# Product-key experts mixed by halves of the tokens, with the up products of the first half among the mixing of the second

## What is computed

```python
def _L0_ffn_ref(x, w_q, keys, expert_down, expert_up, norm_w):
    H, DK, K = (8, 128, 8); NKEYS = 64; NEXP = NKEYS * NKEYS
    xn = _rmsnorm(x, norm_w)
    q = (xn @ w_q.T).reshape(b, t, H, 2, DK)
    sim1 = jnp.einsum('bthd,hkd->bthk', q[..., 0, :], keys[:, :, 0, :])
    sim2 = jnp.einsum('bthd,hkd->bthk', q[..., 1, :], keys[:, :, 1, :])
    s1, i1 = jax.lax.top_k(sim1, K)
    s2, i2 = jax.lax.top_k(sim2, K)
    all_idx = (i1[..., :, None] * NKEYS + i2[..., None, :]).reshape(b, t, H, K * K)
    all_sc = (s1[..., :, None] + s2[..., None, :]).reshape(b, t, H, K * K)
    fs, pk = jax.lax.top_k(all_sc, K)
    fi = jnp.take_along_axis(all_idx, pk, axis=-1)
    wd, wu = expert_down[fi], expert_up[fi]
    hidden = jax.nn.gelu(jnp.einsum('btd,bthkd->bthk', xn, wd), approximate=False)
    hidden = hidden * jax.nn.relu(fs)
    return jnp.einsum('bthk,bthkd->btd', hidden, wu)
```

## Time and profile before

| | us |
|---|---|
| median of 3 runs | 486.81 (485.98 to 500.19) |
| the profiled execution, its own time | 488.01 |
| its span in the trace | 486.2 |
| PE busy | 453.0 (93%) |
| DVE busy | 285.0 (59%) |
| ACT busy | 180.9 (37%) |
| mean granted clock of PE | 0.965 of 2.4 GHz |

### The profile page before, as it was taken

How to read it: one execution, slowest core, us unless ns; L and a number is a source line. 1 busy time by engine, 2 the same in 40 slices (tenths; PEclk the granted TensorE clock), 3 DMA queues, 4 the chain that set the end, 5 groups by cost and what they waited for, 6 DMA issues and landing times.

```text
span 486.2 us, 8648 instructions
## 1 busy us (share of the span) xinstructions
PE 453.0 (93%) x3217; PEld 320.0 (66%) x3217; DVE 285.0 (59%) x967; ACT 180.9 (37%) x444; POOL 6.4 (1%) x9
## 2 busy tenths in 40 slices
PE   4999999999999899978899899899899999979997
PEld 3645555455455588856758788788646778767774
DVE  7266676676667654787689889500336554435243
ACT  2446665755665602777223220000024333223110
POOL 4000000000000000000000000000000000000000
PEclk9999999999999999999999995689899999988999
DMA  8400001000004906100089278000291000000000
GB/s 296 141 2 2 0 1 45 1 0 0 0 0 160 359 6 266 82 1 1 2 263 329 74 239 195 0 0 1 51 379 54 0 1 1 0 1 1 0 1 22
DMA packets 21694, 36.20 MB, mean 74 GB/s; under 512 B 1696, under 2 KB 18209, under 8 KB 21025
## 3 DMA queue, kind: packets, MB, share of 16 engines
q1 hardware_dynamic: 21664, 35.82, 22.9%
HBM read 35.55 MB, written 0.26 MB: 74 GB/s over the span
## 4 chain that ended last, share of the span: by engine, by line
issue 44%; PE 37%; DVE 15%; ACT 2%; POOL 1%; DVEq 0%; DMA 0%; POOLq 0%
PE bank L824 6%; PE bank L985 6%; PE bank L890 4%; PE bank L865 3%; PE bank L870 2%; PE bank L999 2%; PE bank L814 1%; DVE region_a L1538 1%; PE bank L879 1%; DVE region_a L1596 1%; PE bank L793 1%; PE bank L1003 1%; DVE region_a L1535 1%; DVE region_g L1604 1%; PE bank L382 1%
## 5 line engine op out<-in xcount | busy, mean ns | idle before, releaser
L1062 ACT ACTIVATE region_g<-bank,nm_new 128x512 f32<-128x512 f32 x64 | 43.4, 683 | 40.8 <-DVE nm_new L1326 40.0
L1321 DVE CUSTOM_DVE_ANT_0 bank<-bank,bias_h 128x512 f32<-128x512 f32 x64 | 43.0, 713 | 7.5 <-issue 7.5
L526 PEld LDWEIGHTS bank<-ident,region_g 128*128 128x128 f32 x264 | 28.2, 140 | 24.8 <-issue 12.1
L526 PE MATMUL bank<-ident,region_g 128*128 128x128 f32 x264 | 36.2, 280 | 0.8 <-ACT region_d L1043 0.8
L543 PE MATMUL bank<-region_d,region_a 128*64 128x256 f32 x288 | 35.0, 385 | 0.0
L566 PE MATMUL bank<-region_a,qT 64*128 64x512 f32 x128 | 34.7, 618 | 0.0
L324 ACT ACTIVATE root<-var 128x2 f32<-128x2 f32 x6 | 1.2, 203 | 84.0 <-DVE var L334 84.0
L824 PE MATMUL bank<-region_u,region_g 128*128 128x256 f32 x128 | 30.4, 403 | 1.5 <-issue 1.5
L1043 ACT COPY region_d<-bank 128x512 f32<-128x512 f32 x50 | 27.6, 587 | 11.0 <-PE bank L526 11.0
L824 PEld LDWEIGHTS bank<-region_u,region_g 128*128 128x128 f32 x128 | 26.0, 204 | 5.6 <-issue 1.6
L814 PE MATMUL bank<-region_a 64*128 64x32 bf16 x768 | 27.2, 249 | 2.2 <-DVE region_a L1596 2.2
(11 more groups left out here) (317 smaller groups left out, 807.4 us busy)
## 6 DMA issues: line engine op xcount, KB each, us to landing
region_d<-in_downT SPq DMA_DIRECT2D x2, 2048.0 KB, 10.2
region_u<-in_up SPq DMA_DIRECT2D x2, 2048.0 KB, 12.3
region_a<-in_ctx SPq DMA_DIRECT2D x1, 3072.0 KB, 16.1
region_d<-in_w_q SPq DMA_DIRECT2D x1, 2048.0 KB, 12.2
region_d<-in_ctxT SPq DMA_DIRECT2D x1, 2048.0 KB, 9.9
region_d<-in_ctxT SPq DMA_DIRECT2D x2, 1024.0 KB, 16.0
region_u<-in_wg SPq DMA_DIRECT2D x1, 1728.0 KB, 8.2
region_u<-in_wu SPq DMA_DIRECT2D x1, 1728.0 KB, 13.2
```

Source lines behind the costliest of these rows:

```text
L526: mm = nc.tensor.transpose(bank[4 + e][:, k * P:(k + 1) * P], prob[:, u % 2, e, k * P:(k + 1) * P], ident[:, :])
L1062: nc.scalar.activation(prob[:, u % 2, e, :], bank[2 * s + e][:, :], ACT.Exp, scale=-1.0, bias=nm_new[:, p, t, e:e + 1], accum_out=l_blk[:, ...
L1321: ins = nc.vector.tensor_tensor_reduce(bank[2 * s + e][:, :], bank[2 * s + e][:, :], bias_h[:, t, :], -1.0, 3e38, ALU.add, ALU.min, accum_ ...
```

## The change

A pass now makes the weights of 32 tokens of one tile: the upper 64 rows of the array take 16 tokens of that tile's first 64, the lower rows the 16 that lie 64 later. So passes 1 to 4 finish token tile 0 and passes 5 to 8 tile 1. For this `chosen` holds each token's 64 entries twice, the turning takes six transposes into two banks, and `chosenT` is copied by two instructions on 64 partitions each.

On PE passes 1 to 4 stay in a loop. Then PE waits until tile 0 is weighed, and passes 5 to 8 are written out with seven up products of tile 0 in each (`BESIDE = 7`): two after every 24 mixing matmuls, one after the last 24. Four up products of tile 0 and the 32 of tile 1 follow; before those of tile 1 PE waits for the last weighing.

On DVE the three multiplications by score pieces become one instruction on 1536 elements, the two of `weigh` one on 1024; the eight passes are written out, and the one-hots of pass 2 come ahead of the wait for the GELU.

```diff
+HALF = P // GS // 2
+BESIDE = 7
...
-        chosen = part(region_a, 3584, 3 * P).rearrange("p (s n) -> p s n", s=3)
+        chosen = part(region_a, 3584, 6 * P).rearrange("p (s t c n) -> p s t c n", s=3, t=TT, c=2)
...
                     for k in range(3):
-                        mm = nc.tensor.transpose(bank[2][:, k * P:(k + 1) * P], chosen[:, k, :], ident[:, :])
+                        for t in range(TT):
+                            mm = nc.tensor.transpose(bank[2 + t][:, k * P:(k + 1) * P],
+                                                     chosen[:, k, t].rearrange("p c n -> p (c n)"), ident[:, :])
...
-            with pe.Fori(0, P // GS // 2) as i:
+            def up_rows(t, e, last):
+
+                return nc.tensor.matmul(bank[6 + t][:, 0:D], lhsT=hidden[:, e, t * P:(t + 1) * P],
+                                        rhs=up[:, e, :], start=False, stop=last)
+
+            def mix_weights(g, n, each):
+
+                pe.wait_ge(hot_ready, n)
+                pe.wait_ge(hidden_ready, n)
+                for s in range(GS):
+                    for w in range(3):
+                        for k in range(2):
+                            own = slice(64 * k, 64 * k + 64)
+                            mm = nc.tensor.matmul(
+                                bank[2 + 2 * g + k][:, :].rearrange("p (h s) -> p h s", h=ET)[:, :, s],
+                                lhsT=hot_lo[own, g, :, s], rhs=hot_hi[own, g, w, :, s], start=w == 0, stop=w == 2)
+                            if s == GS - 1 and w == 2:
+                                mm.then_inc(mixw_psum, 1)
+                    each(s)
...
+            with pe.Fori(0, HALF // 2) as i:
                 two = pe.snap(i * 2)
                 for g in range(2):
...
+                    mix_weights(g, two + (g + 1), nothing)
             pe.wait_ge(gelu_ready, ET // 2)
-            pe.wait_ge(hidden_ready, 2 + P // GS)
+            pe.wait_ge(hidden_ready, 2 + HALF)
             pe.wait_ge(up_in, 32)
-            for t in range(TT):
-                for e in range(ET):
-                    mm = nc.tensor.matmul(bank[6 + t][:, 0:D], lhsT=hidden[:, e, t * P:(t + 1) * P],
-                                          rhs=up[:, e, :], start=False, stop=e == ET - 1)
+            for q in range(HALF):
+
+                def one_of_first_half(s):
+                    if s % 4 == 3:
+                        for e in range(s // 2 - 1, min(s // 2 + 1, BESIDE)):
+                            up_rows(0, q * BESIDE + e, False)
+
+                mix_weights(q % 2, HALF + q + 1, one_of_first_half)
+            for e in range(HALF * BESIDE, ET):
+                up_rows(0, e, e == ET - 1)
+            pe.wait_ge(hidden_ready, 2 + 2 * HALF)
+            for e in range(ET):
+                mm = up_rows(1, e, e == ET - 1)
             mm.then_inc(y_psum, 1)
...
-                for w in range(3):
-                    ins = nc.vector.tensor_tensor(hot_hi[:, g, w], hit_hi[:, g], over(2 + w, ET), ALU.mult)
-                ins.then_inc(hot_ready, 1)
...
+                nc.vector.tensor_tensor(hot_hi[:, g], hit_hi[:, g].unsqueeze(1).to_broadcast([P, 3, ET, GS]),
+                                        chosen_h[:, 2:5, bass.ds(at, GS)].unsqueeze(2).to_broadcast([P, 3, ET, GS]),
+                                        ALU.mult).then_inc(hot_ready, 1)
+
+            def weigh(n):
+
+                dve.wait_ge(mixw_psum, 2 * n + 2)
+                t, at, b = n // HALF, n % HALF * GS, 2 + 2 * (n % 2)
+                own = hidden_sh[:, t, :, :, at:at + GS]
+                nc.vector.tensor_tensor(own, banks[:, b:b + 2, :].rearrange("p k (h s) -> p k h s", h=ET),
+                                        own, ALU.mult).then_inc(hidden_ready, 1)
 
             one_hots(0, 1, 0)
+            one_hots(1, 2, GS)
             dve.wait_ge(gelu_ready, ET // 2)
...
+            for n in range(2 * HALF):
+                weigh(n)
+                if n + 2 < 2 * HALF:
+                    one_hots(n % 2, n + 3, (n + 2) * GS)
```

More of the change, by code:

```diff
@@ L70, in sem @@
             return ctx.enter_context(nc.semaphore(name))
-        bank = [ctx.enter_context(nc.psum_tensor(f"bank{i}", [P, 512], F32)) for i in range(8)]
+        banks = ctx.enter_context(nc.psum_tensor("bank", [P, 8, 512], F32))
+        bank = [banks[:, i, :] for i in range(8)]
         ident = sb("ident", [P, P])
@@ L157, in build @@
         hidden = region_g[:, :].rearrange("p (h t) -> p h t", h=ET)
+        hidden_sh = region_g[:, :].rearrange("p (h t s n) -> p t s h n", h=ET, t=TT, s=2)
         hot_lo = part(region_a, 0, GS * P).bitcast(BF16).rearrange("p (b l s) -> p b l s", b=2, s=GS)
@@ L806, in _, with nothing @@
+            def nothing(s):
+                pass
+            with pe.Fori(0, HALF // 2) as i:
                 two = pe.snap(i * 2)
                 for g in range(2):
-                    pe.wait_ge(hot_ready, two + (g + 1))
-                    pe.wait_ge(hidden_ready, two + (g + 1))
-                    for s in range(GS):
-                        for w in range(3):
-                            for t in range(TT):
[L813 to L818, removed]
+                    mix_weights(g, two + (g + 1), nothing)
@@ L1555, in _ @@
             step(ins)
-            nc.vector.tensor_scalar(chosen[:, 2, :], best.rearrange("p t k -> p (t k)"), 0.0, None, ALU.max
+            nc.vector.tensor_scalar(chosen[:, 2], best.unsqueeze(2).to_broadcast([P, TT, 2, 64]), 0.0, None, ALU.max
                                     ).then_inc(chosen_ready, 1)
@@ L1574, in _ @@
             for k in range(2):
-                nc.vector.tensor_copy(chosen[:, k, :], split_i[:, k].rearrange("p t k -> p (t k)")
+                nc.vector.tensor_copy(chosen[:, k], split_i[:, k].unsqueeze(2).to_broadcast([P, TT, 2, 64])
                                       ).then_inc(chosen_ready, 1)
             dve.wait_ge(chosenT_psum, 1)
-            step(nc.vector.tensor_copy(chosenT, bank[2][:, 0:3 * P].rearrange("p (s n) -> p s n", s=3)))
+            for k in range(2):
+                own = slice(64 * k, 64 * k + 64)
+                turned = banks[own, 2:4, 0:3 * P].rearrange("p t (s c n) -> p s t c n", s=3, c=2)[:, :, :, k, :]
+                ins = nc.vector.tensor_copy(chosenT[own].rearrange("p s (t n) -> p s t n", t=TT), turned)
+            step(ins)
             for k in range(2):
```

1 line of the change is left out of this document (removed).

## The result

The changed kernel takes 489.14 us (median of 20 runs, 485.76 to 491.44) against 486.87 before (20 runs). The ratio, which leaves out two of the 20 runs before that took 500.2 and 500.3 us at a mean granted clock of 0.935, is 1.0062, 95% interval 1.0031 to 1.0092: slower by 0.6%, which is 3 us. The profiled execution took 491.09 us with a span of 489.3; before it was 486.2.

The account below looks back on a forecast made before the run. PE bounds the stage, with DVE setting the pitch from the third pass. 15.4 + 12.9 + 12.0 + 4.8 + 15.6 + 1.8 = 62.5, and 0.6 ahead, is +1.9 us: 488.7 us, range 482.5 to 493.

Parts of the forecast that it names:

- the sum: PE's stage from first mixing matmul to last up product, 62.5 us, plus 0.6 ahead: 63.1 against 61.2, +1.9 us.
- Ahead of the mixing: Before PE's first mixing matmul: six transposes for three and wider DVE instructions add 0.6 us, bounds 0.4 to 1.2.
- elsewhere: A dip of the granted clock somewhere else, its place shifting with the program: chance 0.03.
- Passes 1 to 4: Mixing: merged DVE instructions cut the pitch from 3.68 to about 3.47 us; pass 3 starts at 7.2, pass 4 ends at 14.1.
- the moved pause: PE's 1.46 us wait before the up products moves between passes 4 and 5, which then starts at 15.4; gain 0.
- rival 3: DVE's merged multiplication loses its rate and takes 1.75 us, 2.6 later in all: about 491.3 us, chance 0.08.
- Changes of mode: Passes 5 to 8: each of 16 groups of up products costs PE 0.30 us, 4.8 in all, bounds 0 to 6.7.
- Rival 1: Passes 5 to 8: the tiling-mode changes are hidden, costing 0 to 1.5 us instead of 4.8: about 484.5 us, chance 0.32.
- The clock: Half clock at pass 5's start, back after 5 us: 1.6 us lost plus 0.2 for slower mode changes, where 2.8 before.
- Rival 2: The clock stays at half through passes 5 to 8, +10.4 us and up to 4.8 more: about 501 us, chance 0.07.
- The stage: PE from first mixing matmul to the end of the up products: 62.5 us forecast against 61.2 before.

Follow-up runs that it names:

- 16 groups in 64 rows: Changed kernel, each up product among the mixing made as two 64-row matmuls in the mixing's mode, lower half's sum left out: 485.9 us, ratio 0.9970.
- 64-row runs: Changed kernel with up products among the mixing as two 64-row matmuls: grouped as in the change 485.9 us, each up product alone 483.9 us.
- 28 groups: Changed kernel with the seven up products of a pass each alone among the mixing: 496.6 us, from four of its 7 runs; the others 505.5 to 506.5.
- four groups with late wait: Changed kernel, all seven up products behind a pass's last mixing matmul, wait for pass 4's weighing moved behind pass 5's mixing: 480.7 us, ratio 0.9872.
- no interleaving: Changed kernel with no up product among the mixing (BESIDE = 0), token halves and merged DVE instructions kept: 481.0 us, ratio 0.9870.
- four groups: Changed kernel with all seven up products of a pass behind its last mixing matmul, wait before pass 5 as it was: 483.8 us, ratio 0.9938.
- merged DVE only: Kernel before with only the merged multiplication and weighing and DVE's passes written out; tokens and PE's order as before: 484.1 us, ratio 0.9954.

## Why the prediction was right

- **Direction and size.** Forecast +1.9 us, measured +2.3 by the medians and +3.0 by the ratio. In the profiled executions the span grew 3.1. The runs of both kernels spread by the clock, so the ends are worth a look too: from the lowest run to the lowest it is +3.7 (482.05 to 485.76), and the highest of the change, 491.44, is 2.7 above the 488.75 of before (its highest but for the two at 500). The direction is the same at both ends.
- **Luck.** The total comes closer than the account of it. Of the 3.1 in the profiled executions 1.4 are what the sum names (0.9 in the stage and 0.5 ahead, against 1.3 and 0.6). The other 1.7 came from a half-clock stretch that the sum doesn't have.
- **Ahead of the mixing**, +0.6 forecast: +2.19 in the profiled execution. Of this 0.5 is the transposes and the wider instructions (turning 0.17 later, the next down products 0.33 behind that), as the sum had it. The other 1.7 is a half-clock stretch that I had only as a chance of 0.03 "elsewhere". 10 of the change's 20 runs have the mean clock of the profiled one, 0.975, and they are its slowest. That all of them had this stretch is not shown: the profiled run with 16 groups in 64 rows has the same mean clock, and its clock is 1.00 there (277.5 to 281.0).
- **Passes 1 to 4 and the moved pause.** Pass 3 starts 7.14 after the start (7.2 forecast), pass 5 at 15.42 (15.4). L1628 holds DVE 0.87, as interpolated; rival 3 is out.
- **Changes of mode.** 0.30 a group forecast, 0.31 measured in the change, 0.29 to 0.31 by the number of groups. The three parts are as forecast too: 0.11 going in, 0.10 for the first weights, 0.10 coming out., which are f32 on both sides, carried over to bf16. Rival 1 is out. That the mode itself is the cause was argued, and is now shown by the 64-row runs.
- **The clock.** It came back after 4.2 us and 1.3 were lost; forecast 5 and 1.8. Rival 2 didn't happen in the change, but it is real: it happened with 28 groups. The reason that I gave against it, that half of the time is full f32 work, doesn't hold in general.
- **The stage**: 62.5 forecast, 62.1 measured. A record is 0.216 us and not 0.214, as the sum has it from the earlier trace rows with 112 distances for 111; this adds less than 0.3 to the 27.4 us of up products, and the clock cost 2.6 before and not 2.8. The profiled time was 491.1 against 489.9; the difference is the stretch at 277.4 less what the clock in the stage lost less.

## What to carry to other kernels

When two kinds of matmul that use the array in different row tilings are interleaved, count the groups: each cost 0.3 us here, with one, two or four a pass, so fill a pause with one large group and not with many small ones. Compare that with what the pause is worth: here the pauses were 0.28 us a pass, and a split that lets one half's work cover the other's last wait gave all of the gain without interleaving. Put a wait where the first instruction that needs it stands, not ahead of the pass; and first take instructions out of the engine that sets the pitch, which shortened the stage by 2 us with nothing else changed.

## What was not expected of the hardware

- The granted clock can stay at 0.50 for 48 us while PE is busy all the time (47.99 of 48.00), when up products and mixing alternate in 28 groups. With the up products in the mixing's mode it came back within 4 us of pass 5's start in the profiled execution, and the mean clocks of all 10 runs (0.981 to 0.985) leave no room for such a stretch.
- The part behind the stage, which is the same in all kernels, takes 137.6 us with no half-clock stretch before its last 2 us (four groups with late wait, and no interleaving), 139.3 with one (four groups), 140.9 with two (merged DVE only) and 142.2 with three (before, and the change). So the same work takes up to 4.6 us more through the clock alone, and part of the 6 us by which the fastest forms lead is of this kind: their stages account for 4.2 to 4.6 less 0.5 ahead. Whether the moment at which the stage ends decides it isn't shown. Each figure is of one profiled execution, and the runs of one kernel differ as much (482.1 to 488.8 before).
